# Latent attention scores with full contraction rows, and TensorE going two steps per round

## The chip, the cores and the metric

The kernel runs on one core of a Trainium2 chip. The metric is the device time of one execution in microseconds (us), here the median of three runs. Differences of under 0.5% are about what a measurement of this kernel can't tell from no change.

## The reference

The input is x, 4 sequences of 512 tokens, 256 wide, fp32. Six layers follow one another, each added to x after a layer norm: a routed expert layer (64 experts), gated linear attention, the routed layer again, a dense layer of 8 experts, latent attention, and the dense layer again. The change touches only the latent attention:

```python
q = (x @ W_q).reshape(B, S, 16, 128)             # W_q: 256 x 2048
latent = x @ W_kv_down                           # 64 wide
kv = (latent @ W_kv_up).reshape(B, S, 16, 128)   # keys and values are the same
scores = einsum('bhqd,bhkd->bhqk', q, kv) / sqrt(128)
probs = softmax(scores)
out = einsum('bhqk,bhkd->bhqd', probs, kv) @ W_o
```

## The kernel before

W_kv_up is folded into the other two weights ahead of time. `absorb` turns x into a query of 64 numbers for each head, to be multiplied with the 64-wide latent, and `mix` turns 64 outputs of each head into the 256-wide result. Two heads make a pair: 8 pairs for each of the 4 sequences, 32 in all.

A *step* s is one tile of 128 queries of one pair, against all 512 keys: 4 steps for each pair, 32 for each sequence (`PER`), 128 in all (`NS`). For each step:

1. **Scores** (TensorE, `scores`). The product is made from a high and a low part in fp32r. `qa` holds, for head hh, the high part of the query in its own 64 rows and the low part in the other 64; `latT` holds the latent's high and low part, each twice, once in each half of the rows. The first product (L1980) takes all 128 rows, query (high and low) by latent high. The second (L1982) takes only the 64 rows of the query's high part, by latent low. Both heads together are four matmuls of 512 columns, in order high, high, low, low; the last two lie in different halves of TensorE's rows.
2. **Maximum** (VectorE, `row_max`, L2180) of both heads, then **exponential** and row sum (ScalarE, `exps`, L2085, one for each head), the **reciprocal** (VectorE, `inverse`, L2176), and **scaling** of the probabilities (GpSimd, L2127, one for each head).
3. **Transposes** (TensorE, `probs_transposed`, L1990): four of 128x128 for each head into PSUM, `TLAG` = 2 steps after the scores. There is one PSUM bank for each head (`ps_p`). Head 0's is emptied by VectorE (`pT_copy`, L2187), head 1's by ScalarE (`pT_copy`, L2093). The transposes of the next step wait for these copies (`pT_ready`).
4. **Values** (TensorE, `values`, L2001): for one key tile, latent by transposed probabilities, head 0 into PSUM rows 0 to 63 and head 1 into rows 64 to 127, 64 output columns of the array each, `VLAG` = 6 steps after the scores. After the fourth, VectorE copies the result (`oT_copy`, L2191).

TensorE's order in one step is: scores of s, transposes of s-2, values of s-6, and then at most one piece of other work. These pieces (queries of a later pair L1959, the mix of the sequence before L1966, transposed x L1936, latent L1943 and L1950) use one PSUM bank, `m_bank`, that has to be filled and emptied in turn; the tables `Q_AT`, `MIX_AT`, `TR_AT`, `LATT_AT`, `LATK_AT` say at which step of a sequence each stands.

Each engine runs its own list in order. ScalarE's list for one step is: `exps(s)`, then `pT_copy(s-2)`, then the bank's copies. VectorE's is: `inverse(s-1)`, `row_max(s)`, `pT_copy(s-2)`, `oT_copy`, copies of the bank, statistics of the next sequence. GpSimd only scales. The stage issues no DMA of its own.

Of the kernel before, what the change touches and what calls it, by code (L numbers as in the profile page):

```python
# [17 lines left out]
TB = T // P  # L18
# [1829 lines left out]
def latent_attention(nc, k):  # L1848


    PER = PAIRS * TB
    NS = B * PER
    NP = B * PAIRS
    TLAG, VLAG = 2, 6
    RING, OSLOTS = 3, PAIRS + 2
    Q_AT = {1: None, 3: 2, 6: 3, 11: 4, 16: 5, 20: 6, 22: 7, 27: PAIRS, 31: PAIRS + 1}
    del Q_AT[1]
    MIX_AT = {8: (0, 0), 9: (0, 1), 13: (1, 0), 14: (1, 1)}
    TR_AT = {18: 0, 24: 1}
    LATT_AT, LATK_AT = 29, 1  # L1860

    stats_done, ln_steps = k.sem("m_stats_steps"), k.sem("m_ln_steps")
    xn_ready = k.sem("m_xn_ready")
# [5 lines left out]
    pT_ready = [k.sem(f"m_pT_ready{hh}") for hh in range(2)]  # L1869
    v_ready, o_copied = k.sem("m_values_ready"), k.sem("m_o_copied")  # L1870

    def misc_of(s):

        b, l = s // PER, s % PER
        if l == LATK_AT and b > 0:
            return ("lat", b)
        if l in Q_AT and b * PAIRS + Q_AT[l] < NP:
            return ("q", b * PAIRS + Q_AT[l])
        if l in MIX_AT and b > 0:
            return ("mix", b - 1, MIX_AT[l][0])  # L1880
        if l in TR_AT and b + 1 < B:
            return ("tr", b + 1, TR_AT[l])
        if l == LATT_AT and b + 1 < B:
# [4 lines left out]
    for s in range(NS):  # L1888
        if misc_of(s) is not None and misc_of(s) not in uses:
            uses.append(misc_of(s))  # L1890
# [5 lines left out]
    with ExitStack() as ctx:  # L1896
# [22 lines left out]
        def rows_of(hh):  # L1919
            return slice(hh * LAT, (hh + 1) * LAT)  # L1920

        @block.tensor
        def _(pe):
# [46 lines left out]
            def scores(s):  # L1970
                pair, t = s // TB, s % TB
                b, q, to = s // PER, qa[pair % RING], ps_s[s % 2]
                if t == 0:
                    pe.wait_ge(bank_free, use_at[("q", pair)] + 1)
                    pe.wait_ge(bank_free, use_at[("latT", b)] + 1)
                if s >= 2:
                    pe.wait_ge(p_ready, 2 * (s - 1))
                cols = slice(t * P, (t + 1) * P)
                for hh in range(2):
                    pe.matmul(to[:, hh, :], q[:, hh, cols], latT[b % 2][0][:, :], start=True, stop=False)  # L1980
                for hh in range(2):
                    pe.matmul(to[:, hh, :], q[rows_of(hh), hh, cols], latT[b % 2][1][rows_of(hh), :],  # L1982
                              start=False, stop=True).then_inc(s_ready, 1)

            def probs_transposed(s, hh):
                pe.wait_ge(scaled, 2 * s + hh + 1)
                if s:
                    pe.wait_ge(pT_ready[hh], s)
                for t in range(TB):
                    ins = pe.transpose(ps_p[hh][:, t, :], prob[s % 3][:, hh, t * P:(t + 1) * P], k.ident[:, :])  # L1990
                ins.then_inc(pT_raw[hh], 1)

            def values(pair, t):
# [15 lines left out]
            queries(0)  # L2009
            queries(1)  # L2010
            latent_rows(0)
            for s in range(NS + VLAG):
                b, l = s // PER, s % PER
                if s < NS:
                    scores(s)
                if 0 <= s - TLAG < NS:
                    for hh in range(2):
                        probs_transposed(s - TLAG, hh)
                if s >= VLAG:
                    values((s - VLAG) // TB, (s - VLAG) % TB)  # L2020
                if s >= NS:
                    continue
                if l == LATK_AT and b > 0:
                    latent_rows(b)
                if l in Q_AT and b * PAIRS + Q_AT[l] < NP:
                    queries(b * PAIRS + Q_AT[l])
                if l in MIX_AT and b > 0:
                    half, t = MIX_AT[l]
# [5 lines left out]
                if l in TR_AT and b + 1 < B:  # L2034
                    transposed(b + 1, TR_AT[l])
                if l == LATT_AT and b + 1 < B:
                    latent_columns(b + 1)
            take(("mix", B - 1, 0))
            for t in range(2):
# [7 lines left out]
        def _(act):  # L2047
# [24 lines left out]
            def q_high(pair):  # L2072
                full(("q", pair))
                if pair >= RING:
                    act.wait_ge(s_ready, 2 * TB * (pair - RING + 1))
# [23 lines left out]
            latT_high(0)  # L2099
            q_high(0)  # L2100
            q_high(1)
            for s in range(NS + TLAG):
                b, l = s // PER, s % PER
                if s < NS:
                    exps(s)
                if s >= TLAG:
                    pT_copy(s - TLAG)
                if s >= NS:
                    continue
                if l in Q_AT and b * PAIRS + Q_AT[l] < NP:  # L2110
                    q_high(b * PAIRS + Q_AT[l])
                if l in TR_AT and b + 1 < B:
                    xT_copy(b + 1, TR_AT[l])
                if l == LATT_AT and b + 1 < B:
                    latT_high(b + 1)
                if l == 9 and b + 1 < B:
                    log_variance(b + 1)
                if l == 10 and b + 1 < B:
                    inverse_deviation(b + 1)

        @block.gpsimd
        def _(pool):
# [8 lines left out]
        def _(dve):  # L2131
# [44 lines left out]
                dve.reciprocal(rinv[s % 2][:, :], rsum[s % 2][:, :]).then_inc(inv_ready, 1)  # L2176

            def row_max(s):
                dve.wait_ge(s_ready, 2 * (s + 1))
# [21 lines left out]
            q_low(0)  # L2201
            q_low(1)
            lat_copy(0)
            for s in range(NS + VLAG):
                b, l = s // PER, s % PER
                if 1 <= s <= NS:
                    inverse(s - 1)
                if s < NS:
                    row_max(s)
                if 0 <= s - TLAG < NS:  # L2210
                    pT_copy(s - TLAG)
                if s >= VLAG and (s - VLAG) % TB == TB - 1:
                    oT_copy((s - VLAG) // TB)
                if s >= NS:
                    continue
                before, lb = (s - 1) // PER, (s - 1) % PER
                if s and lb in Q_AT and before * PAIRS + Q_AT[lb] < NP:
                    q_low(before * PAIRS + Q_AT[lb])
                if l == LATT_AT + 1 and b + 1 < B:
                    latT_low(b + 1)  # L2220
                if l == LATK_AT + 1 and b > 0:
                    lat_copy(b)
                if l in (10, 15) and b > 0:
                    add_out(b - 1, l // 15)
                if b + 1 < B:
                    if l < TB:
                        statistics(b + 1, l)
                    if l == TB:
                        for j in range(TB):
                            moments(b + 1, j)  # L2230
                    if 12 <= l < 12 + TB:
                        normalise(b + 1, l - 12)
            add_out(B - 1, 0)
            full(("mix", B - 1, 1))
            x = k.X[:, B * TB - 2:B * TB, :]
# [112 lines left out]
```

## Time and profile before

| what | value |
|---|---|
| time, median of 3 runs | 2085.37 us (2079.65 to 2087.36) |
| the profiled execution | 2093.63 us, span 2091.8 us |
| TensorE (PE) busy, whole span | 83% |
| VectorE (DVE), ScalarE (ACT), GpSimd (POOL) busy | 58%, 35%, 38% |
| mean granted TensorE clock | 0.887 |
| latent attention, first scores to last addition | about 1421 to 1958 us of the span |

Times in the rows are microseconds from the span's start. PE is a matmul, PEld a load of its stationary operand. A matmul's row begins about when its weights begin to load and ends when its modelled result has landed, so rows overlap: how long a matmul occupies TensorE is read from start to start, not from its length.

### The profile page before, as it was taken

The numbers are of one execution on the slowest core, as the hardware profiler recorded it, in microseconds if no ns is written. First come the engines' busy times: TensorE is split into PE (matmuls) and PEld (weight loads), VectorE is DVE, ScalarE is ACT, GpSimd is POOL, SyncE is SP. The second block draws the span as 40 slices with busy tenths as digits, with TensorE's granted clock in tenths as the row PEclk, the third lists the DMA queues.
The fourth block names the chain that finished last, engine by engine and source line by source line (L and its number), as shares of the span: only waits on it lengthen the run. The fifth ranks groups of instructions, "written<-read, shape, count | busy, mean of one in ns | idle before, by whom it ended". The sixth has DMA issues, their size and how long they took to land. (4 is left out here: it accounts for less than half of the span.)

```text
span 2091.8 us, 28820 instructions
## 1 busy us (share of the span) xinstructions
PE 1743.2 (83%) x7754; PEld 1115.7 (53%) x7754; DVE 1206.5 (58%) x3086; ACT 722.5 (35%) x1772; POOL 797.5 (38%) x1047
## 2 busy tenths in 40 slices
PE   3777996379898999677699848878999999999798
PEld 2544664137566667544466536654445455554577
DVE  5882222384747463488422268865765666647488
ACT  1322332324233241123233311114654655646211
POOL 3554443432322110055444376604553544545000
PEclk9898998678787887588899968888999999999999
DMA  7303995211010000121199722200000000000000
GB/s 227 101 11 88 298 304 171 68 31 31 28 31 16 16 1 0 51 61 55 34 297 290 218 83 77 77 5 0 1 1 1 1 1 1 1 1 1 3 18 21
DMA packets 82844, 142.25 MB, mean 68 GB/s; under 512 B 15306, under 2 KB 42802, under 8 KB 82754
## 3 DMA queue, kind: packets, MB, share of 16 engines
q1 hardware_dynamic: 53058, 90.79, 14.2%
q0 software_dynamic: 15360, 37.77, 6.2%
q10 hardware_dynamic: 14336, 12.59, 2.0%
q8 instruction: 44, 0.72, 0.1%
q14 instruction: 46, 0.38, 0.1%
HBM read 122.23 MB, written 18.87 MB: 67 GB/s over the span
## 5 line engine op out<-in xcount | busy, mean ns | idle before, releaser
L2127 POOL TENSOR_TENSOR sb_m_prob<-sb_m_prob,sb_m_rinv 128x512 f32<-128x512 f32 x256 | 260.8, 1040 | 315.3 <-DVE sb_m_rinv L2176 315.3
L2085 ACT ACTIVATE sb_m_prob<-m_ps_s,sb_m_nmax 128x512 f32<-128x512 f32 x256 | 173.8, 683 | 210.3 <-DVE sb_m_nmax L2180 210.3
L1205 POOL DMA_INDIRECT sb_c_rows<-slot_rows,sb_c_at x192 | 194.9, 1015 | 74.9 <-issue 48.7
L2180 DVE TENSOR_REDUCE sb_m_nmax<-m_ps_s 128x2 f32<-128x1024 f32 x128 | 156.4, 1222 | 114.7 <-PE m_ps_s L1982 113.8
L1184 DVE TENSOR_TENSOR sb_e_h<-sb_e_sg,e_ps_gu 96x176 f32<-96x176 f32 x128 | 42.6, 333 | 259.1 <-ACT sb_e_sg L1160 259.1
L1122 PE MATMUL e_ps_gu<-e_wgu,sb_e_xT 128*96 128x352 f32 x512 | 177.5, 469 | 10.9 <-ACT sb_e_xT L1154 10.6
L1097 POOL DMA_INDIRECT sb_e_x<-xn_rows,sb_e_index x128 | 121.4, 948 | 103.3 <-POOL sb_e_index L131 97.6
L1990 PE MATMUL m_ps_p<-sb_ident,sb_m_prob 128*128 128x128 f32 x1024 | 143.3, 281 | 8.6 <-ACT sb_m_pT L2093 6.9
L2001 PE MATMUL m_ps_v<-sb_m_pT,sb_m_lat 128*64 128x512 f32 x512 | 137.4, 617 | 0.9 <-DVE sb_m_oT L2191 0.9
L1990 PEld LDWEIGHTS m_ps_p<-sb_ident,sb_m_prob 128*128 128x128 f32 x1024 | 110.1, 141 | 44.3 <-issue 40.4
L1139 PE MATMUL e_ps_y<-e_wdn,sb_e_hT 96*96 96x256 f32 x512 | 131.3, 380 | 0.0
L1219 DVE SCALAR_TENSOR_TENSOR sb_x<-sb_c_rows,sb_weight,sb_x 128x256 f32 (+1 forms) x192 | 94.5, 492 | 59.7 <-DMA sb_c_rows<-slot_rows,sb_c_at 54.7
L1665 POOL TENSOR_TENSOR sb_g_sq<-sb_g_o 128x256 f32<-128x256 f32 x16 | 10.0, 627 | 286.0 <-ACT sb_g_o L1568 286.0
L840 POOL TENSOR_TENSOR sb_r_hot_tok<-sb_r_hot,sb_token_part 128x384 bf16<-128x384 f32 x64 | 51.5, 826 | 153.8 <-DVE sb_r_posf L888 153.8
L311 PE MATMUL d_ps_e<-sb_d_we_high,sb_d_xT_high 128*128 128x512 f32 x256 | 99.7, 472 | 9.7 <-DVE sb_d_xT_low L433 9.7
L1980 PE MATMUL m_ps_s<-sb_m_latT_high,sb_m_qa 128*128 128x512 f32 x256 | 106.0, 496 | 1.0 <-ACT sb_m_prob L2085 1.0
L1122 PEld LDWEIGHTS e_ps_gu<-e_wgu,sb_e_xT 128*96 128x96 f32 x512 | 74.9, 166 | 49.6 <-ACT sb_e_xT L1154 8.2
L844 POOL TENSOR_SCALAR sb_r_hot_pos<-sb_iota_slot,sb_r_posf 128x96 bf16<-128x96 f32 x192 | 100.6, 541 | 0.0
L719 PE MATMUL s_ps<-sb_r_xnT,sb_sguT 128*128 128x512 f32 (+3 forms) x192 | 95.4, 643 | 1.2 <-DVE sb_x L907 1.0
L2187 DVE COPY sb_m_pT<-m_ps_p 128x512 f32<-128x512 f32 x128 | 87.1, 680 | 2.1 <-PE m_ps_p L1990 2.1
L1166 ACT ACTIVATE sb_e_y<-e_ps_y 96x256 f32<-96x256 f32 x128 | 48.7, 380 | 112.9 <-DMA slot_rows<-sb_e_y 83.3
L311 PE MATMUL d_ps_e<-sb_d_we_low,sb_d_xT_high 128*128 128x512 f32 x256 | 86.3, 421 | 0.0
(260 smaller groups left out, 3665.5 us busy)
## 6 DMA issues: line engine op xcount, KB each, us to landing
e_wgu<-wgu SPq DMA_DIRECT2D x128, 352.0 KB, 4.5
e_wdn<-wdn SPq DMA_DIRECT2D x128, 192.0 KB, 4.3
slot_rows<-sb_e_y ACTq DMA_DIRECT2D x128, 96.0 KB
xn_rows<-sb_r_xn SPq DMA_DIRECT2D x32, 128.0 KB, 1.7
sb_c_rows<-slot_rows,sb_c_at POOLq DMA_INDIRECT x192, 2.7
sb_x<-x SPq DMA_DIRECT2D x1, 2048.0 KB, 8.6
sb_wqT<-wqT SPq DMA_DIRECT2D x1, 2048.0 KB, 8.5
sb_wo<-wo SPq DMA_DIRECT2D x1, 2048.0 KB, 14.5
```

The lines of the kernel that those rows point to most:

```text
L311: ins = pe.matmul(ps_e[j][:, :, :], xTs[u][xpart][:, c, :], we[wpart][:, c, 2 * j:2 * j + 2, :], start=(m == 0), stop=(m == 3 * DC - 1))
L844: ins = pool.tensor_scalar(hot_pos[u][:, j, :], k.iota_slot[:, :], posf[u][:, j:j + 1], None, ALU.is_equal)
L1097: pool.indirect_dma_start(x[u][:, :], None, k.xn_rows[:, :], bass.IndirectOffsetOnAxis(ap=index[u][:, 0:1], axis=0)).then_inc(got[u], 16)
L1122: ins = pe.matmul(ps_gu[v][:, :], xT[v][:, c, :], wgu[(u - 1) % U][:, c, :], start=(c == 0), stop=(c == DC - 1))
L1139: ins = pe.matmul(ps_y[v][:, :], hT[v][:, c, :], wdn[(u - 3) % U][:, c, :], start=(c == 0), stop=(c == 1))
L1205: pool.indirect_dma_start(rows[u][j][:, :], None, k.slot_rows[:, :], bass.IndirectOffsetOnAxis(ap=at[u][:, j:j + 1], axis=0))\
L1980: pe.matmul(to[:, hh, :], q[:, hh, cols], latT[b % 2][0][:, :], start=True, stop=False)
L1990: ins = pe.transpose(ps_p[hh][:, t, :], prob[s % 3][:, hh, t * P:(t + 1) * P], k.ident[:, :])
L2001: ins = pe.matmul(ps_v[rows_of(hh), :], lat[pair // PAIRS % 2][:, t, :], pT[pair % 2][hh][:, t, :], start=(t == 0), stop=(t == TB - 1))
L2085: act.activation(prob[s % 3][:, hh, :], ps_s[s % 2][:, hh, :], ACT.Exp, bias=nmax[s % 2][:, hh:hh + 1], accum_out=rsum[s % 2][:, hh:hh + 1 ...
L2127: pool.tensor_tensor(part, part, rinv[s % 2][:, hh:hh + 1].to_broadcast([P, T]), ALU.mult)\
L2180: dve.tensor_reduce(nmax[s % 2][:, :], ps_s[s % 2][:, :, :], AX, ALU.max, negate=True).then_inc(nmax_ready, 1)
```

## The change

Four things change, all in the latent attention.

- The low product takes all 128 rows too, so that it also adds the product of both low parts. The order becomes high and low for head 0, then high and low for head 1, and the semaphore `s_ready` is raised once for a step, not twice.
- TensorE's list goes by rounds d of two steps: scores(2d), transposes(2d-2), scores(2d+1), transposes(2d-1), then the values of both key tiles (2d-6 and 2d-5), then at most one piece of other work. The tables give rounds; the pieces and their number stay.
- ScalarE's list for a round is exps(2d), pT_copy(2d-2), exps(2d+1), pT_copy(2d-1), then the bank's copies.
- VectorE's list for a round is inverse(2d-1), row_max(2d), pT_copy(2d-2), the bank's copies of the round before, row_max(2d+1), inverse(2d), pT_copy(2d-1), oT_copy, statistics. Two more `oT` buffers are made.

```diff
-    TLAG, VLAG = 2, 6
-    RING, OSLOTS = 3, PAIRS + 2
-    Q_AT = {1: None, 3: 2, 6: 3, 11: 4, 16: 5, 20: 6, 22: 7, 27: PAIRS, 31: PAIRS + 1}
-    MIX_AT = {8: (0, 0), 9: (0, 1), 13: (1, 0), 14: (1, 1)}
-    TR_AT = {18: 0, 24: 1}
-    LATT_AT, LATK_AT = 29, 1
+    NR, RPB = NS // 2, PER // 2
+    RING, OSLOTS = 3, PAIRS + 4
+    Q_AT = {1: 2, 2: 3, 5: 4, 6: 5, 9: 6, 12: 7, 13: PAIRS, 15: PAIRS + 1}
+    MIX_AT = {3: (0, 0), 4: (0, 1), 7: (1, 0), 8: (1, 1)}
+    TR_AT = {10: 0, 11: 1}
+    LATT_AT, LATK_AT = 14, 0
...
                 for hh in range(2):
                     pe.matmul(to[:, hh, :], q[:, hh, cols], latT[b % 2][0][:, :], start=True, stop=False)
-                for hh in range(2):
-                    pe.matmul(to[:, hh, :], q[rows_of(hh), hh, cols], latT[b % 2][1][rows_of(hh), :],
-                              start=False, stop=True).then_inc(s_ready, 1)
+                    ins = pe.matmul(to[:, hh, :], q[:, hh, cols], latT[b % 2][1][:, :], start=False, stop=True)
+                ins.then_inc(s_ready, 1)
...
-            for s in range(NS + VLAG):
-                b, l = s // PER, s % PER
-                if s < NS:
-                    scores(s)
-                if 0 <= s - TLAG < NS:
-                    for hh in range(2):
-                        probs_transposed(s - TLAG, hh)
-                if s >= VLAG:
-                    values((s - VLAG) // TB, (s - VLAG) % TB)
+            for d in range(NR + VLAG // 2):
+                b, e = d // RPB, d % RPB
+                for s in (2 * d, 2 * d + 1):
+                    if s < NS:
+                        scores(s)
+                    if 0 <= s - TLAG < NS:
+                        for hh in range(2):
+                            probs_transposed(s - TLAG, hh)
+                if 2 * d >= VLAG:
+                    for s in (2 * d, 2 * d + 1):
+                        values((s - VLAG) // TB, (s - VLAG) % TB)
...
-            for s in range(NS + TLAG):
-                if s < NS:
-                    exps(s)
-                if s >= TLAG:
-                    pT_copy(s - TLAG)
+            for d in range(NR + TLAG // 2):
+                for s in (2 * d, 2 * d + 1):
+                    if s < NS:
+                        exps(s)
+                    if s >= TLAG:
+                        pT_copy(s - TLAG)
...
+            for d in range(NR + VLAG // 2):
+                s = 2 * d
+                if 1 <= d <= NR:
                     inverse(s - 1)
+                if d < NR:
                     row_max(s)
                 if 0 <= s - TLAG < NS:
                     pT_copy(s - TLAG)
+                if 1 <= d <= NR:
+                    evictions(d - 1)
+                if d < NR:
+                    row_max(s + 1)
+                    inverse(s)
+                if 0 <= s - TLAG < NS:
+                    pT_copy(s - TLAG + 1)
+                if 2 * d >= VLAG and (s + 1 - VLAG) % TB == TB - 1:
+                    oT_copy((s + 1 - VLAG) // TB)
+                if d < NR:
+                    preparations(d)
```

## Rows read from the trace of the kernel before

**Rows 1.** The page: each engine's busy time, share of the span, instructions.

```profile
PE 1743.2 (83%) x7754; PEld 1115.7 (53%) x7754; DVE 1206.5 (58%) x3086; ACT 722.5 (35%) x1772; POOL 797.5 (38%) x1047
```

**Rows 2.** Windows of the stage: its length, engines' busy time (instructions), granted clock.

```profile
1421.30:1443.60 22.30, 17.98 (x74) 10.11 (x73) 15.24 (x28) 11.70 (x30) 11.07 (x11) 0.79 0.00 0
1443.60:1930.70 487.10, 482.63 (x2319) 253.35 (x2318) 311.77 (x490) 273.10 (x677) 245.66 (x242) 1.00 0.00 1
```

**Rows 3.** Timeline of TensorE, a step without other work and the next one's start.

```profile
1610.47 0.73 PE L1980 MATMUL m_ps_s<-sb_m_latT_high,sb_m_qa 128*128 128x512 f32 x2
1611.13 0.50 PE L1982 MATMUL m_ps_s<-sb_m_latT_low,sb_m_qa 64*128 64x512 f32 x2
1611.56 1.09 PE L1990 MATMUL m_ps_p<-sb_ident,sb_m_prob 128*128 128x128 f32 x8
1612.58 1.08 PE L2001 MATMUL m_ps_v<-sb_m_pT,sb_m_lat 128*64 128x512 f32 x4
1613.59 1.98 PE L1959 MATMUL m_bank<-sb_m_xT,sb_absorb 128*128 128x512 f32 x4
```

**Rows 4.** The same timeline, narrower: the second high product; the first value pair.

```profile
1610.80 0.40 PE L1980 MATMUL m_ps_s<-sb_m_latT_high,sb_m_qa 128*128 128x512 f32 x1
...
1612.58 0.65 PE L2001 MATMUL m_ps_v<-sb_m_pT,sb_m_lat 128*64 128x512 f32 x2
```

**Rows 5.** Timeline of TensorE, scores that follow transposes, not values.

```profile
1621.56 0.66 PE L1936 MATMUL m_bank<-sb_ident,sb_m_xn 128*128 128x128 f32 x4
...
1622.61 0.50 PE L1982 MATMUL m_ps_s<-sb_m_latT_low,sb_m_qa 64*128 64x512 f32 x2
```

**Rows 6.** Timeline of the last dense layer, full-row fp32r products of 512 columns.

```profile
2029.77 0.62 PE L311 MATMUL d_ps_e<-sb_d_we_high,sb_d_xT_low 128*128 128x512 f32 x2
...
2030.23 0.62 PE L311 MATMUL d_ps_e<-sb_d_we_high,sb_d_xT_high 128*128 128x512 f32 x2
```

**Rows 7.** Timeline of all engines in the stage's opening, before any values.

```profile
1435.40 1.09 PE L1990 MATMUL m_ps_p<-sb_ident,sb_m_prob 128*128 128x128 f32 x8
1435.53 1.22 DVE L2180 TENSOR_REDUCE sb_m_nmax<-m_ps_s 128x2 f32<-128x1024 f32 x1 [0.94 <-PE m_ps_s L1982]
...
1436.25 0.71 PE L1980 MATMUL m_ps_s<-sb_m_latT_high,sb_m_qa 128*128 128x512 f32 x2
...
1436.79 0.69 ACT L2085 ACTIVATE sb_m_prob<-m_ps_s,sb_m_nmax 128x512 f32<-128x512 f32 x1 [0.83 <-DVE sb_m_nmax L2180]
...
1437.39 1.39 DVE L2158 TENSOR_TENSOR sb_m_qa<-m_bank,sb_m_qa 64x512 fp32r<-64x512 f32 x2
...
1437.50 0.63 PE L1990 MATMUL m_ps_p<-sb_ident,sb_m_prob 128*128 128x128 f32 x4
...
1438.13 0.59 ACT L2093 ACTIVATE sb_m_pT<-m_ps_p 128x512 f32<-128x512 f32 x1
...
1438.87 0.63 PE L1990 MATMUL m_ps_p<-sb_ident,sb_m_prob 128*128 128x128 f32 x4 [0.74 <-ACT sb_m_pT L2093]
```

**Rows 8.** Timeline of all engines in a later step, values between the transposes.

```profile
1649.45 1.09 PE L1990 MATMUL m_ps_p<-sb_ident,sb_m_prob 128*128 128x128 f32 x8
...
1652.19 0.60 ACT L2093 ACTIVATE sb_m_pT<-m_ps_p 128x512 f32<-128x512 f32 x1
...
1652.57 1.09 PE L1990 MATMUL m_ps_p<-sb_ident,sb_m_prob 128*128 128x128 f32 x8
1652.57 2.04 POOL L2127 TENSOR_TENSOR sb_m_prob<-sb_m_prob,sb_m_rinv 128x512 f32<-128x512 f32 x2 [1.09 <-DVE sb_m_rinv L2176]
```

**Rows 9.** Waits in the stage: who for whom, us in total, times, longest.

```profile
PE m_ps_p L1990 <- ACT sb_m_pT L2093: 6.9, 11, 0.7
```

**Rows 10.** Windows of the opening: as Rows 2.

```profile
1436.00:1439.00 3.00, 2.15 (x14) 1.29 (x13) 2.91 (x5) 1.94 (x5) 0.71 (x1) 1.00 0.00 0
1439.00:1442.00 3.00, 1.70 (x11) 1.04 (x11) 2.43 (x6) 1.01 (x3) 2.04 (x2) 1.00 0.00 0
```

**Rows 11.** Timeline of TensorE, transposes at a granted clock of 0.50.

```profile
1427.92 1.97 PE L1990 MATMUL m_ps_p<-sb_ident,sb_m_prob 128*128 128x128 f32 x8
```

More of the change, by code:

```diff
@@ L1870, in latent_attention, with misc_of @@
     v_ready, o_copied = k.sem("m_values_ready"), k.sem("m_o_copied")
-    def misc_of(s):
-        b, l = s // PER, s % PER
-        if l == LATK_AT and b > 0:
+    def misc_of(d):
+        b, e = d // RPB, d % RPB
+        if e == LATK_AT and b > 0:
             return ("lat", b)
[L1877 to L1883, printed above, removed]
+        if e in Q_AT and b * PAIRS + Q_AT[e] < NP:
+            return ("q", b * PAIRS + Q_AT[e])
+        if e in MIX_AT and b > 0:
+            return ("mix", b - 1, MIX_AT[e][0])
+        if e in TR_AT and b + 1 < B:
+            return ("tr", b + 1, TR_AT[e])
+        if e == LATT_AT and b + 1 < B:
             return ("latT", b + 1)
@@ L1887, in latent_attention @@
     uses = [("tr", 0, 0), ("tr", 0, 1), ("latT", 0), ("q", 0), ("q", 1), ("lat", 0)]
-    for s in range(NS):
-        if misc_of(s) is not None and misc_of(s) not in uses:
-            uses.append(misc_of(s))
+    for d in range(NR):
+        if misc_of(d) is not None and misc_of(d) not in uses:
+            uses.append(misc_of(d))
     uses += [("mix", B - 1, half) for half in range(2)]
@@ L2011, in _ @@
             latent_rows(0)
-            for s in range(NS + VLAG):
-                b, l = s // PER, s % PER
-                if s < NS:
-                    scores(s)
-                if 0 <= s - TLAG < NS:
-                    for hh in range(2):
-                        probs_transposed(s - TLAG, hh)
-                if s >= VLAG:
-                    values((s - VLAG) // TB, (s - VLAG) % TB)
-                if s >= NS:
+            for d in range(NR + VLAG // 2):
+                b, e = d // RPB, d % RPB
+                for s in (2 * d, 2 * d + 1):
[7 more added lines that the diff above has]
+                        values((s - VLAG) // TB, (s - VLAG) % TB)
+                if d >= NR:
                     continue
-                if l == LATK_AT and b > 0:
+                if e == LATK_AT and b > 0:
                     latent_rows(b)
[L2025 to L2028, printed above, removed]
+                if e in Q_AT and b * PAIRS + Q_AT[e] < NP:
+                    queries(b * PAIRS + Q_AT[e])
+                if e in MIX_AT and b > 0:
+                    half, t = MIX_AT[e]
                     if t == 0:
@@ L2033, in _ @@
                         ins.then_inc(bank_full, 1)
-                if l in TR_AT and b + 1 < B:
-                    transposed(b + 1, TR_AT[l])
-                if l == LATT_AT and b + 1 < B:
+                if e in TR_AT and b + 1 < B:
+                    transposed(b + 1, TR_AT[e])
+                if e == LATT_AT and b + 1 < B:
                     latent_columns(b + 1)
@@ L2074, in q_high @@
                 if pair >= RING:
-                    act.wait_ge(s_ready, 2 * TB * (pair - RING + 1))
+                    act.wait_ge(s_ready, TB * (pair - RING + 1))
                 for hh in range(2):
@@ L2101, in _ @@
             q_high(1)
-            for s in range(NS + TLAG):
-                b, l = s // PER, s % PER
-                if s < NS:
-                    exps(s)
-                if s >= TLAG:
-                    pT_copy(s - TLAG)
-                if s >= NS:
-                    continue
[L2110 to L2119, printed above, removed]
+            for d in range(NR + TLAG // 2):
+                b, e = d // RPB, d % RPB
+                for s in (2 * d, 2 * d + 1):
[3 more added lines that the diff above has]
+                        pT_copy(s - TLAG)
+                if d >= NR:
+                    continue
+                if e in Q_AT and b * PAIRS + Q_AT[e] < NP:
+                    q_high(b * PAIRS + Q_AT[e])
+                if b + 1 < B:
+                    if e in TR_AT:
+                        xT_copy(b + 1, TR_AT[e])
+                    if e == LATT_AT:
+                        latT_high(b + 1)
+                    if e == 5:
+                        log_variance(b + 1)
+                    if e == 6:
+                        inverse_deviation(b + 1)
         @block.gpsimd
@@ L2178, in row_max @@
             def row_max(s):
-                dve.wait_ge(s_ready, 2 * (s + 1))
+                dve.wait_ge(s_ready, s + 1)
                 dve.tensor_reduce(nmax[s % 2][:, :], ps_s[s % 2][:, :, :], AX, ALU.max, negate=True).then_inc(nmax_ready, 1)
@@ L2203, in _, with evictions, preparations @@
             lat_copy(0)
-            for s in range(NS + VLAG):
-                b, l = s // PER, s % PER
-                if 1 <= s <= NS:
+            def evictions(d):
+                b, e = d // RPB, d % RPB
+                if e in Q_AT and b * PAIRS + Q_AT[e] < NP:
+                    q_low(b * PAIRS + Q_AT[e])
+                if e == LATT_AT and b + 1 < B:
+                    latT_low(b + 1)
+                if e == LATK_AT and b > 0:
+                    lat_copy(b)
+                if e in MIX_AT and MIX_AT[e][1] == 1 and b > 0:
+                    add_out(b - 1, MIX_AT[e][0])
+            def preparations(d):
+                b, e = d // RPB, d % RPB
+                if b + 1 < B:
+                    if e < TB:
+                        statistics(b + 1, e)
+                    if e == TB:
+                        for j in range(TB):
+                            moments(b + 1, j)
+                    if e in (7, 8):
+                        for j in (2 * e - 14, 2 * e - 13):
+                            normalise(b + 1, j)
+            for d in range(NR + VLAG // 2):
+                s = 2 * d
+                if 1 <= d <= NR:
                     inverse(s - 1)
-                if s < NS:
+                if d < NR:
                     row_max(s)
@@ L2211, in _ @@
                     pT_copy(s - TLAG)
[L2212 to L2232, printed above, removed]
+                if 1 <= d <= NR:
[9 more added lines that the diff above has]
+                    preparations(d)
             add_out(B - 1, 0)
```

1 line of the change is left out of this document (removed).

## The prediction

> **What bounds the kernel now.** I read the page first, then the windows of the stage, then timelines in it. The page [rows 1] says TensorE 83% of 2091.8 us; that is a mean over six layers and says little here. The windows of the latent attention [rows 2] say more: between 1443.6 and 1930.7 us TensorE is busy 482.6 of 487.1 us, at clock 1.00 (2.4 GHz). So in this stage TensorE sets the pace, and the question is what it does with the time. One plain step [rows 3] runs from 1610.47 to 1613.59: 3.12 us, of which scores 1.09 (to 1611.56), transposes 1.02, values 1.01.
>
> **What TensorE pays for besides streaming.** Start to start, two full-row fp32r matmuls of 512 columns take 0.46 us [rows 6], 0.23 each. The two 64-row ones of L1982 stand in one row of 0.50 us, and the transposes begin 0.43 us after them [rows 3]: they run side by side, one stream of 0.23 and 0.2 around it. Eight transposes last 1.09 and four 0.66 [rows 3, 5], so one is 0.1075. The four value instructions are two side-by-side pairs: two end at 0.65 and four at 1.08 [rows 3, 4], so a pair is 0.43, and 0.15 of the 1.01 is neither. Streams of a step: 0.46 + 0.23 + 0.86 + 0.86 = 2.41. The rest, 0.71 us, lies at the four places where the shape of the array changes: values to full rows (the second high product starts 0.33 after the first, not 0.23 [rows 3, 4]), full to 64-row, 64-row to transposes, transposes to values. Where scores follow transposes no such time shows: from 1621.56, four transposes (0.43), two high products (0.46), one exposed load (0.1) and the leaving of full rows (0.1) make 1.09, and the trace has 1.05 [rows 5].
>
> The Trainium skill speaks on both sides here. TensorE: Matmul & The Clock Gate, Part 3, says that small-K matmuls in distinct row groups run concurrently; the trace agrees (0.50 us for both), and by that alone this change gives up one stream of 0.23 us in each of 128 steps, +29 us. TensorEngine Tiling, Key Properties, says that changing the tiling mode drains TensorE; the trace agrees with 0.71 us for four changes, but the page has no price.
>
> **Part 1, TensorE's own work.** A round of two steps now costs 8 score streams (1.86), 16 transposes (1.72), 4 pairs of values (1.72), and two changes of shape where there were eight: entering full rows 0.11, to values and back 0.21. Sum 5.62 us against 6.24: it saves 0.62 a round. Bounds: 0.50 (the change to full rows costs its mean share of 0.18, and 0.05 comes back between transposes and scores) to 0.75 (score streams of 0.215, half of a value pair, which has the same 512 columns). I take 0.62, since each term has its own row. The other pieces keep number and shape and still stand between values and scores: 0. Merging s_ready: 0; only the last of both was waited for.
>
> **Part 2, what the moved values no longer cover.** Before, the values lay between transposes(s-2) and transposes(s-1). Now only the scores do. But transposes(s-1) of head 1 wait for ScalarE's pT_copy(s-2), and ScalarE does that only after exps(s), which waits for VectorE's row_max(s), which waits for scores(s). In the plain step of before [rows 8] this copy ends at 1652.79, 3.34 us after the transposes began at 1649.45, and head 1's next transposes are due at 1652.57 + 0.43 = 1653.00: hidden by 0.2 us. That cover is now gone.
>
> The opening of the stage shows the new order, because no values exist there yet [rows 7]: transposes from 1435.40, maximum from 1435.53, scores from 1436.25, exponentials from 1436.79, head 0's next transposes at 1437.50, pT_copy at 1438.13 (ended 1438.72), head 1's next transposes at 1438.87, with ScalarE's copy named as the releaser. The chain row_max(s), exps(s), pT_copy(s-2) is 3.19 us, + 0.15 to the transposes.
>
> Let z be the end of the score stream of step 2d; transposes(2d-2) stream from there. In rows 7 the transposes start at 1435.40, about 0.1 behind the stream's end, so z is 1435.3; head 1's next ones start at z + 3.57, and, their weights loaded, stream at z + 3.67. Without a wait it would stream at 0.86 + 0.93 + 0.43 = z + 2.22. **Wait: 1.45 us a round.** It takes up the smaller one of head 0, which waits for VectorE's copy until about z + 2.3. Low bound 1.2 (the semaphore and load latencies overlap), high bound 1.7 (VectorE or ScalarE begins late, below).
>
> Round: z to head 1's start 3.57, to the values 0.59 (1.02 for eight transposes less 0.43), values 0.43 x 4 + 0.15 = 1.87, entering scores 0.11 + 0.93: 7.07 us. Two plain steps were 6.24. **Net +0.83 a round.** A piece of other work adds the same to either (a query piece four streams of 0.43), at the round's end, where it hides nothing of this chain.
>
> **Part 3, the other queues.** VectorE now has row_max(2d+1) and the bank's copies ahead of inverse(2d). With q_low (1.39 us [rows 7]): copy to z + 2.0, q_low to 3.3, row_max to 4.45, inverse 4.6, GpSimd's 2.04 [rows 8] to 6.75. transposes(2d) are due at z + 7.07, or 1.7 later with the query piece that each round but some of the first and last sequence has: hidden, by 0.3 at the least. inverse(2d+1) stands behind oT_copy, which waits for the values: about z + 7.0; GpSimd ends at 9.1, due at z + 7.07 + 2.3 (head 0 half done by 8.1): hidden. The bank: filled at a round's end, emptied by z' + 3.3 of the next, refilled from z' + 6: hidden. If this cover were missing by 0.5 us in the 30 rounds with queries, it would be +15.
>
> **Sum.** 63 rounds have transposes; in the first two the same wait stands already in the trace of before (the opening took 22.3 us [rows 2] for seven scores and five transposes), which leaves 61 x 0.83 = +50.6. Waits of before in the main stretch, 487.1 - 482.6 = 4.5 us, part of the 6.9 us on this very copy [rows 9], no longer stand apart: -4.5. Opening and closing rounds save a change of shape or two each: -1.5. **+44.6 us.** Against the profiled execution: span 2091.8 to 2136.4, its time 2093.6 to 2138.2; that execution lies 8 us over the median, so from the median 2085.4 + 44.6 = 2130 us.
>
> **Rivals.**
> - *Faster: TensorE stays the bound.* If the copy reached head 1's transposes by z + 2.84 or sooner (wait under the 0.62 saved), the rounds would gain; with no wait at all 63 x 0.62 = -39 and -4.5, 2042 us. It needs 0.8 us out of the 3.3 of the chain, of which 1.2 is the maximum and 1.34 the exponentials of both heads. Rows 7 show the wait in the very order; for it speaks only that rows 8 hide it. 7%.
> - *No difference:* the wait is about as large as what is saved (0.6 to 0.75 a round, through larger savings at shape changes than I count): 2075 to 2096. 8%.
> - *The wait is longer:* VectorE's new order also makes GpSimd or ScalarE late, +0.3 to 0.5 us in half the rounds or more: 2145 to 2160. Part 3 says hidden, with 0.3 at the least. 15%.
> - *The clock falls.* With the waits of 0.5 and 0.95 us TensorE is idle 20% of a plain round. At the lower level (1.2 GHz) a row of eight transposes is 1.97 long [rows 11] against 1.09. If half of each round's 5.3 us of streams ran so, that is +2.65, of which 1.45 would fill the wait: +1.2, 73 us more, 2203. Against it, the opening [rows 10]: TensorE busy 1.70 of 3 us and the clock stayed at 1.00. 8%.
> - *As computed:* 62%, with its own range 2110 to 2148 (wait 1.2 to 1.7: -15, +15; saving 0.50 to 0.73: +8, -7).
>
> Range: 2096 to 2160; below it lie the faster case and most of the unchanged one, above it the clock. Chances, from the same cases: faster by over 0.5% (about what a measurement of this kernel can't tell from no change) 0.07, within 0.5% 0.08, slower by over 0.5% 0.85.
>
> **What the profile of the changed kernel would show.** Part 1: scores of four full-row matmuls, 0.93 start to start behind transposes and about 1.04 behind values; values in a row of 8, about 1.87. Part 2: in the waits a new first row for TensorE, transposes on ScalarE's pT_copy, about 60 times and 0.7 to 0.95 each, beside a smaller one on VectorE's; plain rounds of 7.07 us; TensorE busy nearer 85% than 99% in the stage; the stage 45 us longer. It would be wrong if head 1's transposes follow head 0's at once, if GpSimd's scaling is what they wait for, or if the granted clock leaves 1.00.

## The result, and the profile after

The changed kernel takes 2121.11 us (median of 4 runs, 2117.91 to 2129.44) against 2085.61 (4 runs): ratio 1.0183, 95% interval 1.0162 to 1.0205, 35.5 us slower. The forecast was 2130, in a range of 2096 to 2160.

The first view is that of the scores' tile. It tells how long the stage is, here always taken from the first score matmul to the first matmul of the last mix. Columns: line, engine, operation, count: shortest, median and longest in ns, start of the first and of the last.

```profile
L1981 PE MATMUL m_ps_s<-sb_m_latT_high,sb_m_qa x256: 389/473/797, 1409.0 to 1952.2; 128*128 128x512 f32 x128
...
L1967 PE MATMUL m_ps_s<-sb_mix,sb_m_oT x32: 379/379/380, 1973.7 to 1980.4; 128*128 128x256 f32 x32
```

That is 564.7 us. The kernel before has 1421.3 to 1950.7, 529.4 us. The stage is 35.3 us longer, as much as the whole loss of 35.5. It also begins 12.3 us earlier than in the profile of before, with the same instructions ahead of it. Those stages differ by up to 14 us from one execution to the next (the stage began between 1409.0 and 1422.9 in the 13 profiles of this study), which is why below the length of the stage stands beside each time.

The waits of the changed kernel, in the view of [rows 9]: who waited for whom, us in total, times, longest.

```profile
PE m_ps_p L1990 <- ACT sb_m_pT L2095: 46.3, 63, 0.7
...
PE m_ps_p L1990 <- DVE sb_m_pT L2191: 13.5, 62, 0.5
```

The transposes' wait on ScalarE's copy was there 11 times and is now there 63 times, once in each round with transposes. Ahead of it there is now a smaller one on VectorE's copy of head 0, 62 times.

A plain round (one without other work) late in the stage, all engines, some rows left out, to be set beside [rows 7] and [rows 8]:

```profile
1921.21 1.03 PE L1990 MATMUL m_ps_p<-sb_ident,sb_m_prob 128*128 128x128 f32 x8
1921.41 1.23 DVE L2184 TENSOR_REDUCE sb_m_nmax<-m_ps_s 128x2 f32<-128x1024 f32 x1 [0.35 <-PE m_ps_s L1982]
...
1922.00 0.47 PE L1981 MATMUL m_ps_s<-sb_m_latT_high,sb_m_qa 128*128 128x512 f32 x1
...
1922.67 0.69 ACT L2087 ACTIVATE sb_m_prob<-m_ps_s,sb_m_nmax 128x512 f32<-128x512 f32 x1 [1.79 <-DVE sb_m_nmax L2184]
1922.77 0.40 PE L1982 MATMUL m_ps_s<-sb_m_latT_low,sb_m_qa 128*128 128x512 f32 x1
...
1923.38 0.63 PE L1990 MATMUL m_ps_p<-sb_ident,sb_m_prob 128*128 128x128 f32 x4 [0.21 <-DVE sb_m_pT L2191]
...
1924.01 0.59 ACT L2095 ACTIVATE sb_m_pT<-m_ps_p 128x512 f32<-128x512 f32 x1
...
1924.75 0.63 PE L1990 MATMUL m_ps_p<-sb_ident,sb_m_prob 128*128 128x128 f32 x4 [0.74 <-ACT sb_m_pT L2095]
...
1925.31 1.94 PE L2001 MATMUL m_ps_v<-sb_m_pT,sb_m_lat 128*64 128x512 f32 x8
...
1927.17 0.50 PE L1981 MATMUL m_ps_s<-sb_m_latT_high,sb_m_qa 128*128 128x512 f32 x1
...
1928.20 1.04 PE L1990 MATMUL m_ps_p<-sb_ident,sb_m_prob 128*128 128x128 f32 x8
```

The round is 1928.20 - 1921.21 = 6.99 us, where two plain steps were 6.24 [rows 3]. All seven plain rounds of the main stretch take 6.99 to 7.00. The last score matmul of step 2d+1 starts at 1922.77 and streams 0.23, so the transposes could stream from 1923.00, head 1's from 1923.43 and the values' row could begin at 1923.92 (0.43 for four transposes, 0.06 to leave them). It begins at 1925.31: 1.39 us of wait, head 0's small one included. Without it the round is 5.60. (Eight transposes that wait for nothing take 0.97 to the values in the first experiment below, not 0.92; by that the wait is 1.34 and the round without it 5.65.)

The windows of the main stretch, from transposes(4) to transposes(124), as in [rows 2]:

```profile
1428.40:1950.90 522.50, 464.96 (x2309) 282.31 (x2308) 308.85 (x493) 271.19 (x673) 243.26 (x242) 1.00 0.00 1
```

TensorE is busy 465.0 of 522.5 us, 89%, and the granted clock stayed at 1.00 (2.4 GHz) in this stretch.

### The profile page after: what moved, and what is told of

Read it like the earlier page. It is cut to its first block and busy times, and to the rows that moved or that the text cites. A ratio compares the mean times of both kernels' runs of the same rounds, so it can differ in the third digit from the quotient of the medians.

```text
span 2116.1 us, 28820 instructions
## 1 busy us (share of the span) xinstructions
PE 1722.8 (81%) x7754; PEld 1142.8 (54%) x7754; DVE 1204.5 (57%) x3086; ACT 720.8 (34%) x1772; POOL 796.8 (38%) x1047
## 5 line engine op out<-in xcount | busy, mean ns | idle before, releaser
L1981 PE MATMUL m_ps_s<-sb_m_latT_high,sb_m_qa 128*128 128x512 f32 x256 | 124.0, 484 | 1.5 <-ACT sb_m_prob L2087 1.5
L2001 PE MATMUL m_ps_v<-sb_m_pT,sb_m_lat 128*64 128x512 f32 x512 | 123.8, 605 | 0.9 <-DVE sb_m_oT L2195 0.9
L1982 PE MATMUL m_ps_s<-sb_m_latT_low,sb_m_qa 128*128 128x512 f32 x256 | 101.3, 396 | 0.0
```

What stands on the lines that cost most here:

```text
L1982: ins = pe.matmul(to[:, hh, :], q[:, hh, cols], latT[b % 2][1][:, :], start=False, stop=True)
```

## The experiments

There are three theories. Theory A: the loss is the wait of head 1's transposes on ScalarE's copy, which the moved values no longer cover; the change's savings are real, and the wait takes more. Theory B: VectorE's new list makes GpSimd's scaling late. Theory C: the two side-by-side 64-row products were cheaper than full rows.

| kernel | median us | ratio to before, 95% | stage us | against before's 529.4 |
|---|---|---|---|---|
| changed | 2121.11 | 1.0183, 1.0162 to 1.0205 | 564.7 | +35.3 |
| 1: before, full rows | 2081.53 | 0.9994, 0.9970 to 1.0018 | 523.7 | -5.7 |
| 2: changed, values apart | 2071.39 | 0.9921, 0.9893 to 0.9949 | 516.4 | -13.0 |
| 3: changed, copy first | 2071.98 | 0.9922, 0.9897 to 0.9947 | 509.9 | -19.5 |
| 4: changed, half rows | 2123.95 | 1.0186, 1.0154 to 1.0218 | 565.0 | +35.6 |
| 5: changed, values between | 2063.41 | 0.9897, 0.9866 to 0.9928 | 505.2 | -24.2 |
| 6: changed, a dose | 2127.07 | 1.0197, 1.0167 to 1.0226 | 570.8 | +41.4 |
| 7: 5 with fitting lists | 2050.77 | 0.9820, 0.9786 to 0.9854 | 490.6 | -38.8 |
| 8: 7, late reciprocal | 2047.76 | 0.9817, 0.9789 to 0.9845 | 489.4 | -40.0 |
| 9: 7, half rows | 2058.57 | 0.9865, 0.9837 to 0.9892 | 502.4 | -27.0 |
| 10: 7, values apart | 2073.15 | 0.9931, 0.9905 to 0.9956 | 515.2 | -14.2 |
| 11: 7, the dose | 2045.02 | 0.9794, 0.9767 to 0.9822 | 490.7 | -38.7 |

The stage is read as above, from the one profiled execution of each kernel. Where the length of the main stretch is given below, it is that of its 60 rounds, from the start of scores(6) to that of scores(126).

**1. Full rows alone.** The kernel before with the change's score products. The waits on `s_ready` count one rise a step.

```diff
                 for hh in range(2):
                     pe.matmul(to[:, hh, :], q[:, hh, cols], latT[b % 2][0][:, :], start=True, stop=False)
-                for hh in range(2):
-                    pe.matmul(to[:, hh, :], q[rows_of(hh), hh, cols], latT[b % 2][1][rows_of(hh), :],
-                              start=False, stop=True).then_inc(s_ready, 1)
+                    ins = pe.matmul(to[:, hh, :], q[:, hh, cols], latT[b % 2][1][:, :], start=False, stop=True)
+                ins.then_inc(s_ready, 1)
```

> The kernel before, with the full-row low product alone (order high, low for each head, one s_ready for a step); steps, tables and lists as before. Theory A (the loss is the moved values: they no longer cover ScalarE's copy): full rows alone give back two changes of shape a step, a plain step takes 2.97 us of TensorE's own work instead of 3.12, 128 x 0.15 = 19 us, less up to 0.13 a plain step because the copy then just misses head 1's transposes: 2066 to 2078 us. Theory C (giving up the two side-by-side 64-row products costs one stream of 0.23 a step): 2085 + 29 = 2114.

2081.53 us, no difference that the interval tells; the stage is 5.7 us shorter. Theory C is out: it asked for 2114, and nothing was lost. Theory A's gain was missed too: it asked for 2078 at the most. TensorE's timeline (start, length) shows why:

```profile
1606.64 1.03 PE L1989 MATMUL m_ps_p<-sb_ident,sb_m_prob 128*128 128x128 f32 x8
1607.61 1.08 PE L2000 MATMUL m_ps_v<-sb_m_pT,sb_m_lat 128*64 128x512 f32 x4
...
1609.65 1.15 PE L1989 MATMUL m_ps_p<-sb_ident,sb_m_prob 128*128 128x128 f32 x8
1610.74 1.08 PE L2000 MATMUL m_ps_v<-sb_m_pT,sb_m_lat 128*64 128x512 f32 x4
```

The step is 3.01 us, not 2.97: full rows save 0.11 a step of TensorE's own work, not 0.15. And the next transposes take 1.09 to the values, not 0.97: with the values in between, the copy now misses by 0.12, as was expected, in steps that follow a plain one (44 of the 120 steps of the main stretch take 1.08 or 1.09 there). Even this small saving runs into the chain.

**2. Values apart.** The changed kernel, TensorE's order of before.

```diff
-                if 2 * d >= VLAG:
-                    for s in (2 * d, 2 * d + 1):
+                    if s >= VLAG:
                         values((s - VLAG) // TB, (s - VLAG) % TB)
```

> The changed kernel, with the values of one key tile again behind each step's transposes; full rows, the round tables and the new lists of VectorE and ScalarE stay. Theory A: the wait of transposes on ScalarE's copy (63 times, 46 us in the changed kernel's profile) falls to under 10 us, and the time is that of the first experiment, 2066 to 2078 us. Theory B (VectorE's new list, with the second maximum and the bank's copies ahead of the reciprocal, costs the time through GpSimd): it stays at 2110 to 2125.

2071.39 us: the loss turns into a gain, with VectorE's and ScalarE's new lists kept, so theory B is out. The wait on ScalarE's copy is nearly gone:

```profile
PE m_ps_p L1990 <- ACT sb_m_pT L2094: 1.7, 4, 0.7
```

Its stage is 7.3 us shorter than the first's, whose TensorE order differs only in where the other work stands; the new tables and lists are worth that much together. Which of the two it is was not tried.

**3. Copy first.** TensorE's order stays that of the change; ScalarE's list changes.

```diff
-                for s in (2 * d, 2 * d + 1):
-                    if s < NS:
-                        exps(s)
-                    if s >= TLAG:
-                        pT_copy(s - TLAG)
+                if 2 * d >= TLAG:
+                    pT_copy(2 * d - TLAG)
+                if 2 * d < NS:
+                    exps(2 * d)
+                    exps(2 * d + 1)
+                if 2 * d + 1 >= TLAG:
+                    pT_copy(2 * d + 1 - TLAG)
```

> The changed kernel, with ScalarE's list for a round as pT_copy(2d-2), exps(2d), exps(2d+1), pT_copy(2d-1); TensorE's order stays. Theory A: head 1's copy no longer stands behind the exponentials, so its wait goes; what stays is 0.1 to 0.3 us a round on VectorE's copy of head 0, against a round of 5.62 us of own work: a plain round of 5.75 to 5.95 us, 2055 to 2068 us. Theory B: GpSimd or VectorE is late instead, rounds stay near 6.99 us and the time over 2105.

2071.98 us, 49 us faster than the changed kernel by the order of ScalarE's own list alone. It just missed the expected 2055 to 2068. What stays is seen in its timeline:

```profile
1890.08 1.04 PE L1990 MATMUL m_ps_p<-sb_ident,sb_m_prob 128*128 128x128 f32 x8
...
1892.25 1.06 PE L1990 MATMUL m_ps_p<-sb_ident,sb_m_prob 128*128 128x128 f32 x8 [0.21 <-DVE sb_m_pT L2193]
1893.25 1.94 PE L2001 MATMUL m_ps_v<-sb_m_pT,sb_m_lat 128*64 128x512 f32 x8
```

Both heads' transposes now go together (x8), behind VectorE's copy of head 0. They come 2.17 us after the ones before, where 1.80 (0.80 for transposes, 1.00 for scores by their starts) would do, and their weights are loaded after the wait: about 0.45 a round, where 0.1 to 0.3 was expected. Its waits also name GpSimd's scaling, 27 times for 12.8 us in all. So with the changed kernel's order on TensorE, the place of ScalarE's copy alone decides between a loss and a gain.

**4. Half rows in the change.** The edit of the first, undone in the changed kernel (s_ready again rises twice a step, and its waits count so):

```diff
-                    ins = pe.matmul(to[:, hh, :], q[:, hh, cols], latT[b % 2][1][:, :], start=False, stop=True)
-                ins.then_inc(s_ready, 1)
+                for hh in range(2):
+                    pe.matmul(to[:, hh, :], q[rows_of(hh), hh, cols], latT[b % 2][1][rows_of(hh), :],
+                              start=False, stop=True).then_inc(s_ready, 1)
```

> The changed kernel, with the low product on 64 rows again (order high, high, low, low; two rises of s_ready a step); the rounds and lists of the change stay. Theory A: of the two scores of a round, the first lies ahead of the chain that ends in the wait, and costs 0.16 us more (two changes of shape, one stream less), the second lies inside the wait and costs nothing: 63 x 0.16 = +10 us, 2131. If the second were on the path too, +20, 2141. Theory C (side by side is cheaper): less than 2121.

2123.95 us; the stage is 565.0 against 564.7. All of theory A's +10 is missing. TensorE's timeline of it:

```profile
1605.32 1.03 PE L1981 MATMUL m_ps_s<-sb_m_latT_high,sb_m_qa 128*128 128x512 f32 x2
1606.28 0.51 PE L1983 MATMUL m_ps_s<-sb_m_latT_low,sb_m_qa 64*128 64x512 f32 x2
1606.72 1.09 PE L1991 MATMUL m_ps_p<-sb_ident,sb_m_prob 128*128 128x128 f32 x8
...
1610.19 0.63 PE L1991 MATMUL m_ps_p<-sb_ident,sb_m_prob 128*128 128x128 f32 x4 [0.74 <-ACT sb_m_pT L2096]
1610.75 1.94 PE L2002 MATMUL m_ps_v<-sb_m_pT,sb_m_lat 128*64 128x512 f32 x8
```

From the transposes to head 1's next ones it is 3.47 us here, 3.54 in the changed kernel (1921.21 to 1924.75). What half rows cost comes behind the last score stream (leaving the shape, loading the first transposes' weights), and the chain starts at the end of that stream. So in the changed kernel the full rows bring nothing: what they save lies inside the wait.

**5. Values between.** The values stay in one piece, but behind transposes(2d-2).

```diff
-                if 2 * d >= VLAG:
-                    for s in (2 * d, 2 * d + 1):
-                        values((s - VLAG) // TB, (s - VLAG) % TB)
+                    if s == 2 * d and 2 * d >= VLAG:
+                        for v in (2 * d, 2 * d + 1):
+                            values((v - VLAG) // TB, (v - VLAG) % TB)
```

> The changed kernel, with TensorE's round as scores(2d), transposes(2d-2), values of both key tiles, scores(2d+1), transposes(2d-1), other work. The values stay in one piece, so the own work stays 5.62 us a round. Theory A: the copy has 1.87 us of values to be made in, so the wait ahead of transposes(2d-1) is gone; the one ahead of the next transposes(2d) is covered by the other work, except in about 10 rounds without any and 9 with a short one: 64 x -0.62 + about 24 - 5 of waits of the kernel before: 2058 to 2072 us. If it is not the cover that matters but the merging of the values as such, it stays over 2100.

2063.41 us, as expected: merged values do no harm where they cover the copy. In its waits the next limit shows, GpSimd's scaling:

```profile
PEld m_ps_p L1990 <- POOL sb_m_prob L2131: 28.0, 35, 1.9
...
PE m_ps_p L1990 <- POOL sb_m_prob L2131: 15.3, 31, 1.6
```

**6. A dose.** One small activation more in the changed kernel, between exps(2d) and pT_copy(2d-2). It writes a tile that nothing reads.

```diff
+                        if s % 2 == 0:
+                            act.activation(dose[:, 0:4], k.eps[:, 0:1].to_broadcast([P, 4]), ACT.Copy)
                         pT_copy(s - TLAG)
```

> The changed kernel, with one more small activation (128x4, about 0.2 us) on ScalarE between exps(2d) and pT_copy(2d-2); it writes a tile that nothing reads. Theory A: this place lies on the path in each of some 62 rounds, +0.2 each, +12 us: 2133. Theory B: ScalarE has slack there and the time stays at 2121.

2127.07 us. The stage is 6.1 us longer than the changed kernel's, half of what was expected. ScalarE's timeline tells that the dose was half as large:

```profile
1643.52 0.20 ACT L2088 ACTIVATION_READ_ACCUMULATOR sb_m_prob<-m_ps_s,sb_m_nmax 128x1 f32 x1
1643.61 0.20 ACT L2112 ACTIVATE sb_m_dose<-sb_eps 128x4 f32<-128x4 f32 x1
1643.71 0.59 ACT L2096 ACTIVATE sb_m_pT<-m_ps_p 128x512 f32<-128x512 f32 x1
```

It is 0.20 long, but the copy starts 0.10 behind it. The seven plain rounds take 7.08 to 7.09 us, 0.09 more than in the changed kernel, and the main stretch is 5.4 us longer, 60 x 0.09: what is added there comes back nearly whole. The other 0.7 us lie in the opening, where this execution's clock stood at 0.50 once more, and are not the dose's.

**7 and 8. The lists follow.** On top of the fifth:

```diff
# ScalarE
+                if 2 * d < NS:
+                    exps(2 * d)
+                if 2 * d >= TLAG:
+                    pT_copy(2 * d - TLAG)
+                    pT_copy(2 * d + 1 - TLAG)
+                if 2 * d < NS:
+                    exps(2 * d + 1)
# VectorE
                     evictions(d - 1)
                 if d < NR:
-                    row_max(s + 1)
                     inverse(s)
+                if 2 * d >= VLAG and (s + 1 - VLAG) % TB == TB - 1:
+                    oT_copy((s + 1 - VLAG) // TB)
+                if d < NR:
+                    row_max(s + 1)
                 if 0 <= s - TLAG < NS:
                     pT_copy(s - TLAG + 1)
-                if 2 * d >= VLAG and (s + 1 - VLAG) % TB == TB - 1:
-                    oT_copy((s + 1 - VLAG) // TB)
```

> As the fifth, and the lists follow: ScalarE exps(2d), pT_copy(2d-2), pT_copy(2d-1), exps(2d+1); VectorE inverse(2d) and oT_copy ahead of row_max(2d+1). Theory A: no copy stands behind exponentials that it doesn't have to, no scaling behind a maximum: nearly every round is TensorE's own work, stage 35 to 45 us shorter than before: 2040 to 2052 us. If GpSimd or VectorE bounds instead, 2060 or more.

2050.77 us, as expected, and faster than both kernels. TensorE's main stretch (windows, about transposes(4) to the last) is full again, 448.4 of 451.0 us, and the weight loads' waits on the scaling are down from 28.0 us to 11.8:

```profile
1438.00:1889.00 451.00, 448.44 (x2327) 289.36 (x2327) 311.42 (x498) 272.76 (x677) 246.09 (x242) 1.00 0.00 1
```

```profile
PEld m_ps_p L1990 <- POOL sb_m_prob L2133: 11.8, 18, 1.3
```

The plain rounds are the exception: with no other work behind transposes(2d-1) the seven of them take 6.04 to 6.30 us, where the own work is 5.68 (below).

The eighth puts `inverse(2d-1)` behind `row_max(2d)`:

```diff
-                if 1 <= d <= NR:
-                    inverse(s - 1)
                 if d < NR:
                     row_max(s)
+                if 1 <= d <= NR:
+                    inverse(s - 1)
```

> As the seventh, with inverse(2d-1) behind row_max(2d) on VectorE, not ahead of it. In rounds with little other work the maximum no longer waits for the exponentials of the step before; GpSimd's scaling of 2d-1 starts 1.1 us later but is due 3.8 us into the round. Equal to the seventh within 3 us, if anything up to 3 faster; if GpSimd were the bound, some 5 to 15 slower.

2047.76 us and a stage of 489.4 against 490.6: no difference from the seventh that counts, as expected.

**9 and 10. What the two savings are worth where TensorE sets the pace.** The ninth is the seventh with the fourth's edit. The tenth is the seventh with the values apart, and `oT_copy` again at the end of VectorE's round:

```diff
-                    if s == 2 * d and 2 * d >= VLAG:
-                        for v in (2 * d, 2 * d + 1):
-                            values((v - VLAG) // TB, (v - VLAG) % TB)
+                    if s >= VLAG:
+                        values((s - VLAG) // TB, (s - VLAG) % TB)
```

> The seventh, with the low product on 64 rows again. In the fourth the wait hid this. Here TensorE's own work sets the pace, and both scores of a round are followed at once by transposes: the stream of scores ends no later (two streams side by side save 0.23, entering their shape costs 0.2), but leaving the shape and loading the first transposes' weights, 0.16 to 0.2 us, is bare: 128 x 0.16 = +20 us on the seventh's 2051, 2071. If full rows had no worth of their own: 2051.

> The seventh, with the values of one key tile behind each step's transposes (oT_copy at the end of VectorE's round again). Full rows stay. Two more changes of shape a round, values and full rows, 0.15 to 0.3 together: 64 x 0.15 to 0.3 = +10 to +19 us on the seventh's 2051, 2061 to 2070, near the second's 2071. If merging the values had no worth of its own: 2051.

2058.57 and 2073.15 us; the stages are 11.8 and 24.6 us longer than the seventh's 490.6. So full rows are worth 11.8 / 64 = 0.18 us a round, less than expected, and merged values 24.6 / 64 = 0.38, more. By the 60 rounds of the main stretch alone (11.9 and 24.8 us longer) it is 0.20 and 0.41. TensorE's timelines of the ninth and tenth:

```profile
1611.04 0.73 PE L1981 MATMUL m_ps_s<-sb_m_latT_high,sb_m_qa 128*128 128x512 f32 x2
1611.70 0.49 PE L1983 MATMUL m_ps_s<-sb_m_latT_low,sb_m_qa 64*128 64x512 f32 x2
1612.13 1.09 PE L1991 MATMUL m_ps_p<-sb_ident,sb_m_prob 128*128 128x128 f32 x8
1613.06 0.60 PE L1937 MATMUL m_bank<-sb_ident,sb_m_xn 128*128 128x128 f32 x4
```

```profile
1604.32 1.04 PE L1990 MATMUL m_ps_p<-sb_ident,sb_m_prob 128*128 128x128 f32 x8
1605.29 1.08 PE L2001 MATMUL m_ps_v<-sb_m_pT,sb_m_lat 128*64 128x512 f32 x4
1606.30 0.50 PE L1981 MATMUL m_ps_s<-sb_m_latT_high,sb_m_qa 128*128 128x512 f32 x1
...
1607.34 1.16 PE L1990 MATMUL m_ps_p<-sb_ident,sb_m_prob 128*128 128x128 f32 x8
1608.42 1.08 PE L2001 MATMUL m_ps_v<-sb_m_pT,sb_m_lat 128*64 128x512 f32 x4
```

Half rows: scores 1.09, transposes 0.93 to the next piece; the seventh has 1.04 and 0.87 at the same place (its rows start at 1612.37, 1613.41 and 1614.28): 0.11 a step, 14 us in 128 steps, of which the stage shows 11.8. Values apart: transposes 0.97, values 1.01, scores 1.04, so 6.04 a round if nothing waits, where the seventh's pieces make 0.97 + 1.87 + 1.04 + 0.87 + 0.93 = 5.68. That is 0.36 for two changes of shape, 0.18 each, and 0.11 of a wait in the second transposes (1.08 for 0.97).

**11. The dose where it is covered.** On top of the seventh, on ScalarE:

```diff
                 if 2 * d >= TLAG:
+                    act.activation(dose[:, 0:4], k.eps[:, 0:1].to_broadcast([P, 4]), ACT.Copy)
                     pT_copy(2 * d - TLAG)
```

> The seventh, with the sixth's small activation ahead of pT_copy(2d-2), 0.10 us from start to start as it measured. There it cost 0.10 in each of 64 rounds. Here the values cover the copy: 0, 2048 to 2054. If ScalarE's list bounded whatever TensorE's order: +6, 2057.

2045.02 us, somewhat below the expected 2048 to 2054; the stage is 490.7 us against 490.6: nothing. The same instruction ahead of the same copy lengthens the main stretch by 5.4 us in the changed kernel and by nothing here.

## Why the prediction was right

**The sign and the cause** held as put: the reading that TensorE is full, the chain of maximum, exponentials and copy read in the opening [rows 7], and that it lacks its cover once the values move. 63 waits on that copy stand in the waits of after; removing it by ScalarE's order (3) or by cover (2, 5) turned the loss into a gain, and lengthening it (6) added what was put in, which it did not where the copy is covered (11). The clock did not fall in the main stretch. A plain round was forecast as 7.07 us and is 6.99.

**Part 1, own work, 5.62 us.** The round of after less its wait is 5.60 to 5.65. The two parts of it, measured apart in 9 and 10, are 0.20 and 0.41 a round in the main stretch, together 0.61, where 0.62 was forecast. The split is near what the prediction's mean price gives: 0.71 us for four changes of shape makes 0.18 each, so full rows save four changes and give up two streams a round (0.71 - 0.46 = 0.25), and merged values save two changes (0.36). Only the experiments' own expectations gave full rows more (0.15 or 0.16 a step).

The Trainium skill, TensorEngine Tiling, Key Properties, says that a change of tiling mode drains TensorE. The trace agrees, and gives it a price: two changes cost 0.36 us in the tenth, 0.18 each.

The Trainium skill, TensorE: Matmul & The Clock Gate, Part 3, says that matmuls in distinct row groups run concurrently. By that alone the first experiment would have been 29 us slower; it showed no difference. By the ninth, the stream saved side by side (0.23) is more than paid back in two changes: half rows cost 0.11 a step more.

**Part 2, the wait, 1.45 us.** It measured 1.39. The round's pieces came out a little shorter than their terms: from the end of the score stream to head 1's transposes 3.54 us for 3.57, from there to the values 0.56 for 0.59, values 1.86 and scores 1.03 for 1.87 and 1.04. The net is 0.75 a round, not 0.83; over 61 rounds 45.8, not 50.6. This is half of the 9 us by which the sum was high. (The range of the prediction's main case, 2110 to 2148, is 2108 to 2153 by the terms beside it; nothing hangs on that.)

**The sum's small terms.** From transposes(4) to transposes(124) after takes 522.5 us and before 486.3 (1441.70 to 1928.04), but before has a query piece (1.7) in it that after has made earlier: +37.9. Sixty rounds of 0.75 are 45.0. Taken off that are 5.2 us of idle time in the same stretch of before, forecast as 4.5, and 1.9 us whose source is not known. The opening is where -1.5 was too little: first scores to transposes(4) takes 19.4 us and 20.4 before, with that query piece more in it, 2.7 in favour of the change. The closing is even. 37.9 - 2.7 = 35.2.

In the opening the clock is not the same in the two kernels, which the prediction did not ask about. Windows of before, then of after:

```profile
1421.30:1430.60 9.30, 8.34 (x24) 4.42 (x23) 5.47 (x9) 3.35 (x9) 3.57 (x4) 0.50 0.00 0
```

```profile
1409.00:1411.70 2.70, 2.70 (x8) 2.17 (x8) 0.99 (x2) 0.00 (x0) 0.00 (x0) 0.50 0.00 0
```

The three profiles with 64-row products (before, 4, 9) stand at 0.50 for the first 9 us of the stage, the ten others for under 3 (6 and 8 fall to 0.50 once more, some 6 us in). Why is not shown. It is not what the opening gained: in the first experiment, with before's order and full rows, the clock rose after 2.5 us too, and scores(6) still begin 18.1 us after the first scores, against 18.0 before.

**Part 3** was right that nothing else costs time in the changed kernel. Head 0's small wait on VectorE and a few waits of the transposes' weight loads on GpSimd (15 times, 9.8 us in all) are there, but in the rounds they lie ahead of the end of head 1's copy, and no plain round is over 7.00. What failed was the expectation of the fourth: it put the cost of half rows ahead of the end of the score stream, where the runs showed it behind. The forecast did not rest on that, because it counted the round from the end of the score stream, by the chain.

## What to carry to other kernels

When pieces are merged or moved on a full engine, write down for each piece what is being done elsewhere while it runs, and who needs that next. Here 1.0 us of values covered a copy with 0.2 us to spare; the change saved 0.6 us of own work a round (0.4 of it by moving the values) and laid bare 1.4. The stage's opening, where the moved piece does not exist yet, had the new order in the old profile. Then look at the other engine's list, not only at the moved work: making the copy ahead of the exponentials took off 49 us, more than the whole loss of 35. With the cover put back and the lists fitted, the same merging made the kernel 1.8% faster than the kernel before (the seventh).

## What was not expected

- Changes of the array's shape cost 0.18 us each, nearly the length of a 512-column stream (0.23). Those between values and the rest (0.36 for two, the tenth) and those of the score products (0.11 a step more although a stream of 0.23 is saved, so 0.34 for two, the ninth) cost about the same.
- A short activation of 0.20 us displaces the next by 0.10 only (the sixth); the rows' lengths overlap, so costs are read from start to start.
- The stages ahead of the changed one, with the same instructions, took between 1409 and 1423 us in the 13 profiles. So a change of half a per cent is read from the stage, not from the span.
